# A decoder layer in which the recurrent part's operations change places within a step

## The reference, cut to what matters

```python
# 1. recurrent attention over the 16 positions (axis 0)
k, v, r = (mix of x[l] and x[l-1] by mu_*) @ W*.T
# conv over l with weights exp(-exp(w) * t), of exp(k) and exp(k) * v, by FFT;
# the kernel keeps it as two running sums, Sd and Sn
den = sum_before(exp_k)     + exp_k * exp(u)
num = sum_before(exp_k * v) + exp_k * v * exp(u)
x1 = layernorm(x + (sigmoid(r) * num / den) @ W_out.T)
# 2. cross attention to a context (256 x 192 for each position), 16 heads of width 16
q = x1 @ Wq + bq;  kk = ctx @ Wk + bk;  vv = ctx @ Wv + bv
x2 = layernorm(x1 + softmax(clip(q kk^T / 4, -1e4, 1e4)) vv @ Wo + bo)
# 3. mixture of experts: 16 experts of width 128, 4 groups, the best 2 groups,
#    the best 4 experts of them; beside it two shared experts
scores = sigmoid(x2 @ w_gate.T)
routed = sum over the 4 chosen e of weight_e * (silu(x2 @ w1_e.T) * (x2 @ w3_e.T)) @ w2_e.T
out = layernorm(x2 + routed + silu(x2 @ w1_s.T) * (x2 @ w3_s.T) @ w2_s.T)
```

## Time and profile before

| what | value |
|---|---|
| median of 3 runs | 1160.88 us (1152.69 to 1161.93) |
| the profiled execution | 1156.8 us, of it the span 1154.7 us |
| TensorE | busy for 1061.1 us, 92% of the span |
| VectorE / ScalarE / GpSimd | 772.8 / 695.5 / 635.4 us |
| mean granted TensorE clock | 0.959 |
| chain that ended last | PE 61%, DVE 26%, issue 6%, ACT 3%, DMA 2% |

### The profile page before, as it was taken

One profiled execution on the slowest core, in us unless ns is written; L12 is line 12 of the kernel. 1 busy time (PEld: TensorE's weight loads), 2 busy tenths in 40 slices (PEclk: granted clock), 3 DMA queues, 4 the chain that ended last, 5 costly groups with the idle time before them and its releaser, 6 DMA issues.

```text
span 1154.7 us, 21761 instructions
## 1 busy us (share of the span) xinstructions
PE 1061.1 (92%) x6580; PEld 811.1 (70%) x6580; DVE 772.8 (67%) x1631; ACT 695.5 (60%) x2182; POOL 635.4 (55%) x683
## 2 busy tenths in 40 slices
PE   4688999999999999999899999999999999999993
PEld 2455767776766767767576777877777778787782
DVE  1375686878869787797978765756755444355685
ACT  1157566576666666666466676676777735566532
POOL 5455255657555666656457466674434445566643
PEclk8679899999999999999899999999999999999997
DMA  9604223324433333111312222232223334588765
GB/s 257 205 17 136 89 85 116 108 93 142 137 112 108 103 110 109 52 39 39 117 35 86 75 84 86 87 98 70 75 85 94 97 121 131 175 259 266 230 211 154
DMA packets 97872, 135.39 MB, mean 117 GB/s; under 512 B 11202, under 2 KB 83553, under 8 KB 97760
## 3 DMA queue, kind: packets, MB, share of 16 engines
q1 hardware_dynamic: 84704, 101.53, 29.5%
q0 software_dynamic: 13056, 32.47, 7.8%
HBM read 61.91 MB, written 76.23 MB: 120 GB/s over the span
## 4 chain that ended last, share of the span: by engine, by line
PE 61%; DVE 26%; issue 6%; ACT 3%; DMA 2%; SPq 1%; POOL 0%; DVEq 0%; POOLq 0%; ACTq 0%
PE bS L743 8%; PE bY L800 7%; PE bM L556 7%; PE bT L570 7%; DVE Sc L1279 6%; DVE nmx L1281 4%; PE bU L673 3%; PE bO L764 3%; PE bT L800 3%; PE bU L700 3%; DVE wkv L1256 3%; PE bS L841 3%; PE bC L843 3%; PE bC L782 2%; DVE st L1194 2%
## 5 line engine op out<-in xcount | busy, mean ns | idle before, releaser
L1279 DVE TENSOR_SCALAR Sc<-bS 128x1024 f32<-128x1024 f32 x128 | 155.7, 1217 | 164.1 <-PE bS L743 162.8
L1019 ACT ACTIVATE Sc<-Sc,nmx 128x256 f32<-128x256 f32 x512 | 253.1, 501 | 0.0
L1027 ACT ACTIVATE PT<-bT 128x512 f32<-128x512 f32 x256 | 151.4, 592 | 162.8 <-PE bT L570 161.4
L570 PE MATMUL bT<-idn,Sc 128*128 128x128 f32 x1024 | 168.9, 289 | 10.2 <-ACT PT L1027 9.6
L570 PEld LDWEIGHTS bT<-idn,Sc 128*128 128x128 f32 x1024 | 115.5, 144 | 85.5 <-issue 55.7
L1281 DVE TENSOR_REDUCE nmx<-Sc 128x4 f32<-128x1024 f32 x128 | 156.2, 1220 | 4.4
L743 PE MATMUL bS<-KT,QT 32*128 32x256 f32 x1024 | 150.0, 411 | 4.0 <-DVE Sc L1279 4.0
L1659 POOL DMA_INDIRECT Xs<-x,slots x120 | 119.8, 999 | 35.4 <-issue 18.4
L743 PEld LDWEIGHTS bS<-KT,QT 32*128 32x128 f32 x1024 | 89.8, 189 | 41.4 <-issue 29.9
L1676 POOL DMA_INDIRECT Yt<-PT,dests x86 | 86.0, 1000 | 58.1 <-ACT PT L1098 39.4
L556 PE MATMUL bM<-mix,Wp 128*128 128x256 f32 x384 | 97.7, 400 | 18.9 <-POOL mix L1615 8.0
(11 more groups left out here) (219 smaller groups left out, 2096.3 us busy)
## 6 DMA issues: line engine op xcount, KB each, us to landing
Xs<-yg SPq DMA_DIRECT2D x16, 1768.0 KB, 8.3
xb<-Xs SPq DMA_DIRECT2D x152, 136.0 KB
yg<-Yt SPq DMA_DIRECT2D x30, 512.0 KB, 5.3
W<-w SPq DMA_DIRECT2D x4, 1152.0 KB, 11.8
xTs<-xT SPq DMA_DIRECT2D x16, 256.0 KB, 2.9
x<-x SPq DMA_DIRECT2D x16, 256.0 KB, 3.0
Base<-stg SPq DMA_DIRECT2D x15, 256.0 KB
yg<-Base SPq DMA_DIRECT2D x30, 128.0 KB, 3.4
```

Source lines behind the costliest of these rows:

```text
L570: last = pe.transpose(dst[:, j, t * P:(t + 1) * P], src[:, t, j * P:(j + 1) * P], idn[:, :])
L1019: last = fn(Sc[:, n % 3, m, t, :], Sc[:, n % 3, m, t, :], ACT.Exp, bias=nmx[:, n % 3, m, t:t + 1], accum_out=rs[:, s % 2, t, h:h + 1])
L1027: fn(flat(PT[:, h % RING]), bT[:, :], ACT.Copy).then_inc(a_pt.sem, 1)
L1279: ts(Sc[:, n % 3].rearrange("p m t k -> p (m t k)"), flat(bS[:, :, :]), CLAMP, -CLAMP, ALU.min, ALU.max).then_inc(d_clip.sem, 1)
```

## The change

Five things change, all of them orders within a step. The work is the same.

- VectorE takes both reciprocals of den in one go at the end of slot 7, behind the shared sum, and the rest of the recurrent finish in slot 0 behind the clip. x1's sum and moments go in front of the clip of slot 2, x1's norm to the end of slot 2, x2's norm in front of the clip of slot 3.
- PE computes the context values in slot 0 (with ScalarE's copy) and the recurrent output projection in slot 1.
- VectorE runs parts of the router in front of the product of exp(k) and v in slot 6.
- POOL finishes den before it starts num.
- POOL takes x1's power in front of x2's and of the second part of the sender.

```diff
# PE
-                if 0 <= s < L and g == 1:
+                if 0 <= s < L and g == 0:
                     context_v(s)
-                if A and g == 2:
+                if A and g == 1:
                     project_out(a)
# ScalarE
-                if 0 <= s < L and g == 1:
+                if 0 <= s < L and g == 0:
                     copy_v(s)
# VectorE
-            def invert(s, j):
-                if j == 0:
-                    dve.wait_ge(g_den.sem, g_den.at(s))
-                dve.reciprocal(den[:, j, :], den[:, j, :]).then_inc(d_rden.sem, 1)
+            def invert(s):
+                dve.wait_ge(g_den.sem, g_den.at(s, 2))
+                for j in range(ND):
+                    dve.reciprocal(den[:, j, :], den[:, j, :]).then_inc(d_rden.sem, 1)

             def finish_wkv(s):
                 dve.wait_ge(a_thr.sem, a_thr.at(s))
+                dve.wait_ge(g_den.sem, g_den.at(s))
                 stt(flat(num), flat(thr), 1.0, flat(num), ALU.add, ALU.mult).then_inc(d_num.sem, 1)
-                invert(s, 1)
                 dve.wait_ge(d_rden.sem, d_rden.at(s))
                 dve.wait_ge(d_num.sem, d_num.at(s))
                 tt(num, num, den, ALU.mult).then_inc(d_wkv.sem, 1)
...
                 if T and g == 0:
                     t_chunk(t, 0)
+                if A and g == 2:
+                    add_x(a)
+                if T and g == 3:
+                    norm(1, t, x2[:, t % 2, :, 0:D], x2[:, t % 2, :, 0:D], d_x2)
                 if 0 <= n + 2 < PAIRS:
                     clip(n + 2)
                 if s == -1 and g == 0:
                     fold_bv()
                 if A and g == 0:
-                    invert(a, 0)
+                    finish_wkv(a)
...
                 if T and g == 1:
                     t_chunk(t, 1)
-                if A and g == 1:
-                    finish_wkv(a)
                 if T and g == 2:
                     t_chunk(t, 2)
                     dve.wait_ge(d_z2.sem, d_z2.at(t))
                     moments(1, t, x2[:, t % 2, :, 0:D])
                 if A and g == 2:
-                    add_x(a)
-                if T and g == 3:
-                    norm(1, t, x2[:, t % 2, :, 0:D], x2[:, t % 2, :, 0:D], d_x2)
-                if A and g == 3:
                     norm(0, a, x1, x1, d_x1)
...
                 if T and g == 6:
                     shared_hidden(t, 0)
-                if B and g == 6:
-                    weigh_k(b)
...
                 if T and g == 6:
                     router(t, 1)
+                if B and g == 6:
+                    weigh_k(b)
                 if T and g == 7:
                     router(t, 2)
                     shared_sum(t)
+                if B and g == 7:
+                    invert(b)
# POOL
                 pool.tensor_tensor(den, ek, by, ALU.mult).then_inc(g_den.sem, 1)
+                pool.wait_ge(g_den.sem, g_den.at(s, 1))
+                pool.tensor_tensor(den, den, Sd, ALU.add).then_inc(g_den.sem, 1)
                 pool.tensor_tensor(num, ekv, by, ALU.mult).then_inc(g_den.sem, 1)
-                pool.wait_ge(g_den.sem, g_den.at(s, 2))
-                pool.tensor_tensor(den, den, Sd, ALU.add).then_inc(g_den.sem, 1)
+                pool.wait_ge(g_den.sem, g_den.at(s, 3))
                 pool.tensor_tensor(num, num, Sn, ALU.add).then_inc(g_den.sem, 1)
...
                 pairs(2)
+                if A:
+                    rsqrt(0, a)
                 if T:
                     rsqrt(1, t)
                 send(s - 2, 1)
-                if A:
-                    rsqrt(0, a)
```

## The result

| | median us (lowest to highest) | ratio to before (95% interval) |
|---|---|---|
| before | 1162.0 (1152.7 to 1172.2) | |
| changed kernel | 1165.8 (1160.5 to 1175.2) | 1.0061 (1.0033 to 1.0089) |
| changed kernel, second comparison | 1152.0 (before beside it: 1150.0) | 1.0052 (1.0008 to 1.0095) |

The change made the kernel slower by about 0.6%, 6 to 7 us. I had predicted 1145 us. Executions of one kernel lie up to 2.4% apart (1141.6 to 1168.6 us beside the second comparison), so I read the step from the traces and the total from the ratios, which leave out executions over 1.5% above the fastest. The profiled execution of the changed kernel has a span of 1167.8 us.

A forecast was written before the change was run, and what follows sets the result against it. PE was taken as the bound, in program order. Ordinary steps at -0.85 each gave -8.5; with steps 12 to 15 and the start, -12.3 off the profiled 1156.8 us gave 1144.5, forecast as 1145 us, range 1130 to 1162.

The forecast's parts named there:

- Gain 1, slot 3: Slot 3: PE's wait for the normalised x2 goes, with 0.6 us to spare; minus 1.5 us a step.
- signs of being wrong: PE idle at scores or projection, its R product waiting for L1251, or mean clock in steps 1 to 11 far from 0.96.
- Loss, slot 0: Slot 0: PE waits 1.78 us for the softmax sums' reciprocal, behind the two large reciprocals; plus 1.75 us a step.
- gain 2: Slot 1: PE's transposes no longer wait for ScalarE's last copy of slot 0; minus 0.6 us a step.
- Gain 3, slot 7: Slot 7: router first, its two long VectorE operations shorten and the shared experts' second product starts earlier; minus 0.5 us a step.
- second rival: Little happens (1154): router operations stay long, +0.5 instead of -0.5, or slot 3's 0.6 margin is used up; chance 0.27.
- third rival: Slower (1174): slot 0's wait costs clock, 3.3 us a step in eleven steps; chance 0.08.
- Step 10: Step 10: PE waits in front of the context values for the plan instead of behind them; 0, between -2 and +3.
- Steps 12 to 15: Steps 12 to 15: lose only part of their wait, 0.3 of some 0.6 each; -1.2.
- The start: Before step 0: chain to PE's product at 34.13 ends one reciprocal earlier, -1.6; step 0's earlier x1 sum, -1.
- The clock: Clock falls follow PE's waits; one of 1.5 goes, one of 1.8 comes, so 0, between -8 and +29.
- my -12.3 for the order: Whole kernel: sum of the predicted terms, -12.3 us from the profiled execution of 1156.8 us.

The follow-up runs named there:

- Experiment 2: Kernel before with parts of the change: x2's norm before slot 3's clip 0.998, with K 0.988; product of k and v behind the router 1.005; all three 0.995.
- R: Reciprocal of the softmax sums moved on VectorE from the front of slot 0 to slot 7, ahead of den's two; on the changed kernel, ratio 1.015.
- experiment 3: Changed kernel with K and step 10's routing plan on VectorE spread over slots 0 to 2: ratio 0.983, then 0.982 in more executions.
- the kernel with three edits: Kernel before with x2's norm before slot 3's clip, product of k and v behind the router, and ScalarE's key copy behind slot 3's exponentials: ratio 0.995.
- the best version: Changed kernel with K and step 10's routing plan spread over slots 0 to 2: 1131.7 us, ratio 0.982.
- the kernel with M: Changed kernel with K, R, plan spread over slots 0 to 2, and GpSimd's mixes for v and r moved later in the step: ratio 0.987.
- K: ScalarE's key copy in slot 3 moved behind the slot's first two exponentials: on the changed kernel 1144.7 us, ratio 0.991; on the kernel before 0.993.
- its control: Changed kernel with K, R and step 10's routing plan spread over slots 0 to 2, GpSimd's mixes left in place: ratio 0.989.
- experiment 1: Changed kernel with K (ratio 0.991), with R (1.015) and with both (0.994); kernel before with K alone (0.993).

## Why the prediction was wrong

**The step that failed is "Gain 1, slot 3": minus 1.5.** Its mechanism was right and its worth was not. The wait for x2 went, by a margin of 0.25 us and not of 0.6 (the norm of x2 ends at 466.36, PE turns it at 466.61). I placed PE's next start 1.53 earlier and let that stand for the rest of the step. I asked what is late next for VectorE (0.05 for the clip, measured 0.34) and not for ScalarE, whose chain ended 0.24 us ahead of its user; none of my signs of being wrong names ScalarE. So slot 3 won 1.28 and slot 4 lost 1.16 of it. Experiment 2 shows it from both sides: alone in the kernel before, the edit wins 1.69 in slot 3 and loses 1.56 in slot 4; with ScalarE's copy moved, the pair is worth 1.1. With the measured 1.28 - 1.16 = 0.12 in place of my 1.5, my other terms give 1.15 - 0.12 - 0.5 = +0.53 a step, and the step measured +0.62.

**Loss, slot 0 and gain 2:** right (+1.24 for slots 0 to 2 against +1.15). The wait I wrote as 1.78 is 411.50 - 409.77 = 1.73, and measured 1.71. My cover for the rest of that chain was thin: I let it end at 8.7 us plus up to 1.3 for the mixes and it ends at 9.47 (502.34 + 1.57 - 494.44). It costs nothing in the changed kernel, where PE is itself late, but it is what R ran into.

**Gain 3, slot 7:** right, in mechanism and size: 7.17, L1333 at 0.19, L1347 at 0.28. My second rival turned on this and on the margin in slot 3. Neither failed, and yet its time (1154), with a gain that turned out to be none, was nearer than mine. So was the third rival's (1174), whose mechanism, a loss of clock in steps 1 to 11, did not come.

**Step 10:** I put 0, between -2 and +3; it is +4.5 against the first profile of before and +1.4 against the second. The exchange of waits went about as I had it: PE waited 3.98 us for the late clip before (564.05), and 4.55 for the plan's read (554.25) and 1.58 for the reciprocal (548.88) after. What I left out is low clock: for the same work PE is busy for 51.19 us and not 47.45, 3.7 of the 4.5, with the clock at 0.88 in place of 0.94. The queue in front of the read (9.46 us after the start of the step, before 5.26) could still be shortened, as experiment 3 shows.

**Steps 12 to 15:** I had -1.2. Steps 12 to 14 are 0 (209.41 against 209.40), step 15 is +0.7 (37.78 against 37.07). There was nothing to gain: in the earlier trace rows their idle time is 1.71 us, and 0.42 of it in step 12 and in step 13 is at slot 5.

**The start:** I had -1.6 before step 0. The product at 34.13 starts at 33.51 and 33.91 in the two profiles of the changed kernel, so 0.6 and 0.2 of that came; step 0 begins 1.8 us earlier in one pair and 4.1 later in the other. Steps 0 and 1 took 6.6 less in both pairs, far more than my -1 and -0.85, and by another cause. Windows of steps 0 and 1, before and changed kernel:

```profile
59.43:106.27 46.84, 41.02 (x237) 28.17 (x236) 28.26 (x31) 29.48 (x93) 22.07 (x21) 0.82 0.30 94
106.27:160.62 54.35, 49.82 (x309) 36.27 (x309) 37.93 (x73) 34.30 (x109) 20.82 (x23) 0.91 0.16 48
57.62:102.63 45.01, 38.08 (x237) 26.86 (x236) 28.41 (x31) 29.26 (x93) 22.29 (x21) 0.89 0.32 97
102.63:152.21 49.58, 46.33 (x309) 33.64 (x309) 39.08 (x73) 34.44 (x109) 21.42 (x21) 0.97 0.17 52
```

The same 546 matmuls keep PE busy for 84.41 us and not 90.84, at a higher clock: that is 6.4 of the 6.6. It helped the changed kernel, and I had not forecast it.

**The clock:** I had 0 (-8 to +29). In steps 2 to 9 low clock accounts for 7.9 and 11.3 us in the two profiles of before (390.44 and 393.86, less 8 x 47.82) and 4.7 in both of the changed kernel (392.25 and 392.23, less 8 x 48.44): -3 to -7. The dear falls I priced did not come there. They came in kernels with shorter steps (51.1 us), with R (step 6, 57.3) and once in the kernel before (step 2 of its second profile, 54.35).

**Together**, what is not clock: 8 x 0.62, 0.8 in step 10, 1.1 in step 11 (53.77 against 52.65), 0.7 in step 15 and -0.2 in steps 0 and 1 give +7.4. The executions of the second comparison say the same. Those that the ratio is taken from have 1153.5 us at a mean clock of 0.9711 (nine of the changed kernel) and 1147.5 us at 0.9686 (thirteen of the one before), +6.0. If the missing part of the clock is taken off each (an estimate, as in the prediction: what is missing of the clock is what is lost of the time), 8.7 us remain for the order and -2.7 are the clock. Against my -12.3 for the order, steps 2 to 9 make 11.8 of the difference (8 x 1.47), and gain 1 by itself 11.0 of that. I also took the -12.3 off one profiled execution of 1156.8 us, 5.2 under the median of the 20 executions of the result. The +13 between the first two profiles is not the change's worth: 3.8 of it in steps 12 to 14 and 5.9 in the tail did not repeat (tails: before 250.4 and 249.0, changed 256.2 and 247.9).

**Still open:** why low clock takes slot 1 in nearly every one of steps 2 to 9 in the kernel with three edits and in none of them in the best version. The amount of idle time does not sort them: 1.2 us a step in the first, 2.4 in the best version, and 0.9 in the kernel with M, which ran steps 2 to 8 undisturbed. The first has the output projection in slot 2, the other two in slot 1; but with K and R it is in slot 1 too, and slot 1 fell in three of eight steps, in the same three (5, 7 and 8) in both kernels that have K and R. No run separates these. Nor was GpSimd's part of the change (den first, x1's power first) tried by itself.

## What to carry to other kernels

A wait that is removed is worth only the distance to the next thing that comes due: for each engine list when its result is ready and when it is asked for, over the whole next slot, and look for margins smaller than the gain. Where two chains end within 0.3 us of each other, expect little from moving one: here the steps won 0.1 us or nothing by either and 1.1 by both. A gain in a full step may also lie on an engine that is never the bound: GpSimd's mixes, hidden themselves, lengthened VectorE's two products by 1.3 us in front of TensorE. And read step and time apart: K left the step of the kernel before as it was and still saved 0.7%, by the clock, and the shortest step of all saved nothing over its control that is clear of the noise.

## What the runs showed of the hardware that I had not expected

A VectorE product of 8 columns took as long (0.74 us) as one of 512 columns took once the mixes were gone (0.75 in the mean); it began under a GpSimd product and ended with it. With 512 columns in the same place it took 1.26.

Low clock cost one kernel all that its shorter step had won (46.2 us became 47.9 to 51.1, in two profiles), while steps of 47.47 and 45.97 ran undisturbed for eight and seven steps on end.

In the first profile of the changed kernel, and with K, R or both in it, ScalarE was released late in slot 3 of steps 12 to 15 (in the kernel before with K, in step 15), and TensorE's L843 waited for its copy. In the waits of the changed kernel:

```profile
PE bC L843 <- ACT hTb L1083: 5.5, 6, 1.7
```

ScalarE's copy of turned probabilities (L1027) started 2.0 us after the last recorded start of the transposes it copies, where 0.3 is usual, and the trace names no instruction as what released it. The second profile of the same kernel has nothing of it. The four kernels of experiment 1 all ran on one chip and all have such releases; the fourteen later runs, on four other chips, have none, and neither has the first profile of the kernel before. So it may belong to a chip and not to a kernel. The cause is open.
